# An attention and feed-forward layer on eight cores: the first weight product summed in another order, weight and x loads reordered, six w1 loads issued two steps later

## The reference, cut to what matters

```
x: (4, 4096, 1024) f32
h   = layernorm(x)
q,k,v = the three interleaved thirds of h @ W_qkv.T
attn  = softmax(q @ k.T / sqrt(1024));  out = (attn @ v) @ W_out.T
x   = x + layernorm(out)
f   = gelu(layernorm(x) @ w1 + b1) @ w2 + b2          # 1024 -> 4096 -> 1024
x   = x + layernorm(f * s)                           # s: renormalised top-2 router sum
```

## Time and profile before

| | |
|---|---|
| median of 3 runs | 1098.89 us |
| profiled execution | 1098.99 us, span of its slowest core (core 5) 1097.5 us |
| spans of the 8 cores | 1090.4 to 1097.5 us |
| TensorE busy | 1068.1 us (97%), 5192 matmuls |
| VectorE, ScalarE, GpSimd busy | 345.0, 316.7, 96.7 us |
| DMA | 110.03 MB, mean 100 GB/s |

### The profile page before, as it was taken

The page is one execution under the profiler, slowest core; times in us unless marked ns, Lnnn a source line. Parts: engine busy times, 40 slices in busy tenths (PEclk is TensorE's granted clock), DMA queues, the critical chain, the costliest instruction groups (busy, mean ns, idle before and its releaser), DMA issues.

```text
span 1097.5 us, 14077 instructions; the slowest of 8 cores (1090.4 to 1097.5 us)
## 1 busy us (share of the span) xinstructions
PE 1068.1 (97%) x5192; PEld 493.0 (45%) x5192; DVE 345.0 (31%) x713; ACT 316.7 (29%) x514; POOL 96.7 (9%) x171
## 2 busy tenths in 40 slices
PE   5999999999999999999999997999999999999996
PEld 2554444444444444444444443444444444444444
DVE  0563832333433333334433204023003300330033
ACT  0564432223332222223331222302430243014300
POOL 7220000000000000000000303010000000000000
PEclk9999999999999999999999998999999999999998
DMA  8999973443234445433349999974202220120012
GB/s 121 164 184 209 159 186 66 106 97 86 80 75 102 91 106 106 106 90 79 75 96 148 138 174 174 169 203 118 37 1 75 66 53 1 60 75 20 1 42 74
DMA packets 152867, 110.03 MB, mean 100 GB/s; under 512 B 117600, under 2 KB 128096, under 8 KB 152800
## 3 DMA queue, kind: packets, MB, share of 16 engines
q0 software_dynamic: 31120, 62.94, 29.3%
q1 hardware_dynamic: 121680, 46.20, 20.8%
HBM read 88.69 MB, written 25.17 MB: 104 GB/s over the span
## 4 chain that ended last, share of the span: by engine, by line
PE 89%; DMA 7%; POOL 2%; issue 1%; DVE 0%; SPq 0%; ACT 0%; POOLq 0%; DVEq 0%; ACTq 0%
PE pAll L116 88%; DMA x2s<-xf 4%; DMA wkb<-wk 2%; DMA pT<-pb 1%; PE pAll L120 1%; POOL wkb L110 1%; POOL wqb L110 0%; POOL w2b L110 0%; POOL w1b L110 0%; SPq L112 0%; DVE xf L649 0%; DVE yt L886 0%; ACT ub L588 0%; DVE xf L643 0%; POOLq L983 0%
## 5 line engine op out<-in xcount | busy, mean ns | idle before, releaser
L116 PE MATMUL pAll<-xnT,qt 128*128 128x512 bf16 x1024 | 225.3, 379 | 0.0
L116 PE MATMUL pAll<-xn,pT 128*128 128x512 bf16 x1024 | 223.6, 379 | 0.0
L116 PE MATMUL pAll<-x2T,w1b 128*128 128x512 bf16 x1024 | 222.6, 379 | 0.0
L116 PEld LDWEIGHTS pAll<-xn,pT 128*128 128x128 bf16 x1024 | 100.2, 98 | 120.8
L116 PEld LDWEIGHTS pAll<-xnT,qt 128*128 128x128 bf16 x1024 | 100.1, 98 | 120.9 <-issue 0.3
L116 PEld LDWEIGHTS pAll<-x2T,w1b 128*128 128x128 bf16 x1024 | 99.7, 98 | 120.1 <-issue 1.1
L528 DVE TENSOR_REDUCE nmx<-pAll 128x1 f32<-128x1024 f32 x64 | 78.1, 1222 | 180.0 <-PE pAll L116 180.0
L534 ACT ACTIVATE pb<-pAll,nmx 128x1024 bf16<-128x1024 f32 x64 | 71.3, 1114 | 168.8 <-DVE nmx L528 168.8
L116 PE MATMUL pAll<-w2b,h1b 128*128 128x512 bf16 (+1 forms) x528 | 113.3, 373 | 0.0
L116 PE MATMUL pAll<-w2b,h1a 128*128 128x512 bf16 (+1 forms) x528 | 113.3, 373 | 0.0
L116 PEld LDWEIGHTS pAll<-w2b,h1a 128*128 128x128 bf16 x528 | 51.7, 98 | 59.1
(11 more groups left out here) (86 smaller groups left out, 577.2 us busy)
## 6 DMA issues: line engine op xcount, KB each, us to landing
xf<-xo POOLq DMA_DIRECT2D x16, 512.0 KB, 4.5
x2s<-xf POOLq DMA_DIRECT2D x16, 512.0 KB, 2.9
w1b<-w POOLq DMA_DIRECT2D x8, 1024.0 KB, 23.3
w2b<-w POOLq DMA_DIRECT2D x8, 1024.0 KB, 32.9
x2r<-x2s POOLq DMA_DIRECT2D x16, 512.0 KB, 4.8
y<-yt SPq DMA_DIRECT2D x15, 512.0 KB, 2.7
xn<-xo POOLq DMA_DIRECT2D x16, 256.0 KB, 30.0
xn<-xr POOLq DMA_DIRECT2D x16, 256.0 KB, 56.2
```

The lines of the kernel that those rows point to most:

```text
L116: e.matmul(o, l, m, start=f, stop=s), after, sig)
```

## The change

Six things are edited.

1. Load order. Wq and Wk pieces come as q0 k0, q1 k1, q2 k2, q3 k3 (first column half of Wk), then second-half pieces 0 to 3, then q4 to q7 each with its second-half piece, then first-half pieces 4 to 7, with x tile 0 behind piece 4 and x tile 1 ahead of piece 7.
2. A's first column half is summed over c 0 to 3 in 8 banks and put aside, scaled, as f32 in `part` (in the place of x tiles 16 to 23). Then the whole second half is summed. Then c 4 to 7 of the first half, and the two parts are added: even blocks by one VectorE operation, odd ones by ScalarE into `rest` and an add on GpSimd. TensorE's transpose of tile 1 moves out of A.
3. `fetch_x(16)` waits for these eight results.
4. The first q' group goes tile by tile: 20 pieces of one tile (8 matmuls of 128 columns), four pieces of two tiles (256 columns) and one block of four.
5. `norm_next` calls take other places in the first group; `rot` starts elsewhere.
6. w1 loads 2 to 7 are issued behind `out_proj(12)`, `finish_a(12)` and `finish_b(12)`, not ahead of them.

```diff
--- before.py
+++ after.py
@@ -214,23 +214,33 @@
 
     t_q, t_k, t_x = [], [[], []], []
 
-    def fetch_x(t):
+    def fetch_x(t, after=()):
         src = xo if t < NQT else xr
         row = (t % NQT) * 128
-        t_x.append(DG(xn[:, t * H:(t + 1) * H], src[row:row + 128, :]))
+        t_x.append(DG(xn[:, t * H:(t + 1) * H], src[row:row + 128, :], after))
 
     t_id = DS(ident[:, :], idb[:, :])
     t_b1 = DS(b1f[:, :], b1r[:, :])
+    def fetch_k(c, half):
+        row = slice(c * 128, (c + 1) * 128)
+        k = slice(half * 512, (half + 1) * 512)
+        t_k[half].append(DG(wkb[:, c * H + half * 512:c * H + half * 512 + 512],
+                            wk[row, k]))
+
     for c in range(HC):
-        row = slice(c * 128, (c + 1) * 128)
-        t_q.append(DG(wqb[:, c * H:(c + 1) * H], wq[row, :]))
-        t_k[0].append(DG(wkb[:, c * H:c * H + 512], wk[row, 0:512]))
-    for c in range(HC):
-        row = slice(c * 128, (c + 1) * 128)
-        t_k[1].append(DG(wkb[:, c * H + 512:(c + 1) * H], wk[row, 512:H]))
+        t_q.append(DG(wqb[:, c * H:(c + 1) * H],
+                      wq[c * 128:(c + 1) * 128, :]))
+        fetch_k(c, c // 4)
         if c == 3:
+            for n in range(4):
+                fetch_k(n, 1)
+    for c in range(4, HC):
+        if c == 7:
+            fetch_x(1)
+        fetch_k(c, 0)
+        if c == 4:
             fetch_x(0)
-    for t in range(1, NQT):
+    for t in range(2, NQT):
         fetch_x(t)
 
     t_xT = [None] * NKT
@@ -317,56 +327,90 @@
         t_xT[t] = free[b] = A(lambda e: e.copy(dst, src), [tok])
 
 
+
+
     t_am = [[None] * HC, [None] * HC]
-
-    def am_part(i, half, c, b, aft):
+    part = [at(f"part{i}", 512, F32, R2 + 32 * KB + i * 2 * KB)
+            for i in range(HC)]
+    rest = [at(f"rest{i}", 512, F32, R2 + 48 * KB + i * 2 * KB)
+            for i in range(4)]
+    t_part = [None] * HC
+
+    def am_step(i, half, c, b, first, last, aft):
         return MM(bank[b], wqb[:, c * H + i * 128:c * H + (i + 1) * 128],
                   wkb[:, c * H + half * 512:c * H + (half + 1) * 512],
-                  c == 0, c == HC - 1, aft, c == HC - 1)
-
-    def am_out(i, half, b, done):
-        o = am[:, i * H + half * 512:i * H + (half + 1) * 512]
-        if half == 1 or i % 2 == 0:
-            t = A(lambda e: e.mul(o, bank[b], 0.03125), [done])
+                  first, last, aft, last)
+
+    def scaled(eng, o, b, tok):
+
+        if eng == "act":
+            return A(lambda e: e.mul(o, bank[b], 0.03125), [tok])
+        return V(lambda e: e.tensor_scalar(o, bank[b], 0.03125, None,
+                                           ALU.mult), [tok])
+
+    def am_cols(i, half):
+        return am[:, i * H + half * 512:i * H + (half + 1) * 512]
+
+    for c in range(4):
+        for i in range(HC):
+            tok = am_step(i, 0, c, i, c == 0, c == 3,
+                          [t_q[c], t_k[0][c]] if i == 0 else ())
+            if c == 3:
+                t_part[i] = free[i] = scaled("dve" if i % 2 else "act",
+                                             part[i][:, :], i, tok)
+    for rows in (range(4), range(4, HC)):
+        for c in range(4):
+            for i in rows:
+                aft = [t_k[1][c]] if i == 0 else []
+                if c == 0:
+                    aft.append(free[i])
+                am_step(i, 1, c, i, c == 0, False, aft)
+    for c in range(4, HC):
+        for i in range(HC):
+            tok = am_step(i, 1, c, i, False, c == HC - 1,
+                          [t_q[c], t_k[1][c]] if i == 0 else ())
+            if c == HC - 1:
+                t_am[1][i] = free[i] = scaled("dve" if i % 2 else "act",
+                                              am_cols(i, 1), i, tok)
+    norm_next()
+    last_bank = (0, 1, 2, 3, 4, 5, 7, 6)
+    t_last = [None] * HC
+
+    def last_step(i, c):
+        aft = [t_k[0][c]] if i == 0 else []
+        if c == 4:
+            aft.append(free[last_bank[i]])
+        t_last[i] = am_step(i, 0, c, last_bank[i], c == 4, c == HC - 1, aft)
+
+    def last_out(i):
+
+        b, o, p = last_bank[i], am_cols(i, 0), part[i][:, :]
+        if i % 2 == 0:
+            t_am[0][i] = free[b] = V(lambda e: e.scalar_tensor_tensor(
+                o, bank[b], 0.03125, p, ALU.mult, ALU.add),
+                [t_last[i], t_part[i]])
         else:
-            t = V(lambda e: e.tensor_scalar(o, bank[b], 0.03125, None,
-                                            ALU.mult), [done])
-        t_am[half][i] = free[b] = t
-
-    for c in range(HC):
-        for i in range(HC):
-            tok = am_part(i, 0, c, i, [t_q[c], t_k[0][c]] if i == 0 else ())
-            if c == HC - 1:
-                am_out(i, 0, i, tok)
+            r = rest[i // 2][:, :]
+            free[b] = scaled("act", r, b, t_last[i])
+            t_am[0][i] = G(lambda e: e.tensor_tensor(o, r, p, ALU.add),
+                           [free[b], t_part[i]])
+
+    for c in range(4, 7):
+        for i in range(7):
+            last_step(i, c)
+    norm_apply()
+    transpose_x(0)
     norm_next()
-    for c in range(HC):
-        for i in range(4):
-            aft = [t_k[1][c]] if i == 0 else []
-            if c == 0:
-                aft.append(free[i])
-            tok = am_part(i, 1, c, i, aft)
-            if c == HC - 1:
-                am_out(i, 1, i, tok)
-    norm_apply()
-    for i in range(4, HC):
-        b = i if i < 6 else i - 6
-        for c in range(HC):
-            tok = am_part(i, 1, c, b, [free[b]] if c == 0 else ())
-        if i == 4:
-            transpose_x(0)
-            norm_next()
-            am_out(i, 1, b, tok)
-        elif i == 5:
-            am_out(i, 1, b, tok)
-            norm_next()
-        elif i == 6:
-            am_out(i, 1, b, tok)
-            transpose_x(1)
-        else:
-            norm_next()
+    for i in range(7):
+        last_step(i, 7)
+        if i == 0:
+            last_out(0)
             norm_apply()
-            am_out(i, 1, b, tok)
-    t_amm = tok
+    for c in range(4, HC):
+        last_step(7, c)
+    t_amm = t_last[7]
+    for i in (1, 6, 3, 2, 5, 4, 7):
+        last_out(i)
 
 
     t_v, t_o = [], []
@@ -380,7 +424,7 @@
             wo[c * 128:(c + 2) * 128, :].rearrange("(c p) o -> p c o", p=128),
             [t_amm]))
     for t in range(NQT, NKT):
-        fetch_x(t)
+        fetch_x(t, t_am[0] if t == NQT else ())
     t_rw = DG(rwb[:, :], rwr[:, :])
 
     t_qt, t_s = {}, {}
@@ -391,7 +435,7 @@
 
 
     t_qs = [None] * NQT
-    rot = [2]
+    rot = [0]
 
     def next_free():
         b = rot[0] % 6
@@ -444,33 +488,55 @@
         free[b] = A(lambda e: e.copy(o, bank[b]), [tok, t_qs[4], t_qs[8]])
         t_bm.append(free[b])
 
-    norm_at = {0: (4, 5, 6), 1: (0, 3, 6), 3: (4, 7)}
+
+
+    norm_at = {1: (0, 3, 6), 3: (4, 7)}
     for g in range(NQG):
         toks = []
         if g == 0:
-            three = [next_free() for j in range(3)]
-            q_part(0, 0, three[0], 0, 2)
+            first = [(4, 0), (5, 1), (6, 3), (7, 2), (0, 4), (1, 5)]
+            for j, b in first[:3]:
+                q_part(0, j, b, 0, 1)
+            transpose_x(1)
+            q_part(0, 7, 2, 0, 1)
+            norm_next()
+            norm_next()
+            norm_apply()
+            for j, b in first[:4]:
+                q_part(0, j, b, 1, 1)
+            q_part(0, 0, 4, 0, 2)
             transpose_x(2)
-            transpose_x(3)
+            q_part(0, 1, 5, 0, 2)
+            for j, b in first:
+                q_part(0, j, b, 2, 1)
+                if j == 4:
+                    transpose_x(3)
             norm_next()
-            q_part(0, 1, three[1], 0, 2)
-            q_part(0, 2, three[2], 0, 2)
-            for j, b in enumerate(three):
-                q_out(0, j, b, q_part(0, j, b, 2, 2), toks)
-            transpose_after = (2, 4, 5, 6)
+            for n, (j, b) in enumerate(first):
+                q_out(0, j, b, q_part(0, j, b, 3, 1), toks)
+                if n in (1, 3):
+                    norm_next()
+                if n == 2:
+                    transpose_x(4)
+            transpose_x(5)
+            q_out(0, 2, 0, q_part(0, 2, 0, 0, 4), toks)
             norm_next()
-            transpose_x(4)
-        else:
-            transpose_after = (0, 2, 4, 6)
+            transpose_x(6)
+            norm_apply()
+            q_part(0, 3, 1, 0, 2)
+            transpose_x(7)
+            q_out(0, 3, 1, q_part(0, 3, 1, 2, 2), toks)
+            norm_next()
+            rot[0] = 3
         if g == 2:
             norm_apply()
-        for j in range(3 if g == 0 else 0, HC):
+        for j in range(HC if g else 0):
             if j in norm_at.get(g, ()):
                 norm_next()
             b = next_free()
             q_out(g, j, b, q_part(g, j, b, 0, 4), toks)
-            if g < 3 and j in transpose_after:
-                transpose_x(4 * (g + 1) + transpose_after.index(j))
+            if g < 3 and j in (0, 2, 4, 6):
+                transpose_x(4 * (g + 1) + j // 2)
```

(6 more changed lines are left out.)

## The result

The changed kernel takes **1103.18 us** (median of 9 runs, 1100.58 to 1109.56), the kernel before 1098.74 on the same chip (9 runs): a ratio of 1.0047, 95% interval 1.0028 to 1.0066. It is within 2%, as I had given it 0.96, but it is slower beyond that interval, and 6 us above the top of my range (1097.0). The profiled execution took 1103.18 us for a span of 1101.6 on its slowest core, which is core 5 again. So core 5 can be held against core 5: +4.1 us. It is no typical core, though: the other seven have spans of 1091.9 to 1099.4, and cores 1, 2 and 3 are 0.9 to 4.0 us faster than before.

What follows compares the result with a forecast made beforehand. TensorE was taken as the bound nearly everywhere, with the DMA engines busy through the first 145 us. Core 5: 1097.5 - 8.7 + 1.8 = 1090.6; another core perhaps slowest at 1091.0; forecast 1092.4 us, range 1089.2 to 1097.0.

Steps and rivals of the forecast that it cites:

- stall ahead of `out_proj(15)` and its clock: TensorE's 6.69 us wait before `out_proj(15)` and the lowered clock behind it go: -8.7 us on core 5.
- start of the first scores: TensorE loses its lead from A by tile 8's transpose and lags: +1.8 us on core 5.
- waits for w2 in the first ffn2: The last w2 piece still lands in time for ffn2: cost 0, up to 2 us for the range.
- the slack is between 0 and 2: a cost of 0: w2's 4.5 us of slack, with need 8.7 us earlier and the stream 4 to 6 us quicker.
- They start at 607.9 as before, or 1 to 3 us later.: w1 pieces 2 to 7 wait for `pT(15)`, which may be delayed 1 to 3 us by tile 12's two stores.
- I put that at 4 to 6 us: Gain of the w2 stream from losing the pause after 660.5 and tile 12's 0.75 MB: 4 to 6 us.
- ScalarE's burst: First q' group: six bank copies and more come in a lump, so VectorE idles some 2 us after tile 7's Ln.
- The last keys: Before chunk 3 of the first scores: a TensorE lead wins at most 1.0 us on core 5, 0 on core 2.
- The lowered clock: Rival: the wait at tile 8 lowers TensorE's clock, costing 2.0 to 2.25 us, total 1094.6; chance 0.23.
- Slower: Rival: `uT(15)`, queued against w1 and w2, lands late and `out_proj(15)` waits again, up to 1100.7; chance 0.04.
- Absorbed: Rival: VectorE keeps up, TensorE's lead of up to 1.4 us is lost at the last keys, 1090.7; chance 0.27.
- The sign that I had named: If `out_proj(15)` waits for a DMA, or ffn2 for w2, the account of the second place is wrong.

Runs made afterwards that it cites:

- start alone: The changed kernel with edit 6 undone, the w1 loads back in their old place: 1103.86 us, ratio 1.0051 to the kernel before.
- w1 alone: The kernel before with only edit 6, w1 loads 2 to 7 issued later: 1095.31 us, ratio 0.9973.
- Experiment 5: The kernel before with the last four of B's 16 blocks summing one of eight chunks (28 matmuls left out, B wrong there): 1097.79 us, ratio 0.9998.
- repaired start: Edits 1 to 5 with `rot` 4 in place of 3 and the statistics of tiles 8 and 9 ahead of tile 7's application: 1100.96 us, ratio 1.0018.

## Why the prediction was wrong

Core 5, the step as predicted and as the trace has it:

| step | predicted | measured |
|---|---|---|
| stall ahead of `out_proj(15)` and its clock | -8.7 | -8.9 |
| start of the first scores | +1.8 | +4.4 |
| waits for w2 in the first ffn2 | 0, up to 2 | +8.7 |
| span | -6.9 | +4.1 |

The measured -8.9 is the start of the first ffn2, 695.20 against 699.67, with the lag of 4.4 taken out. The +8.7 is how much longer the first ffn2 takes: the 8.0 of waits, and 0.16 us more at each of the four than the idle time says.

**The step that failed: "the slack is between 0 and 2: a cost of 0".** It failed in two places.
- "They start at 607.9 as before, or 1 to 3 us later." They started 9.85 us later. 4.71 of it is the lag: `pT(15)` is issued at 601.81 instead of 597.10. The other 5.1 is the transpose, landing after 15.3 us instead of 10.2. Its issue, and its landing after and before:
```profile
601.81 10.35 SPq L112 DMA_TRANSPOSE pT<-pb  x1
```
```profile
pT<-pb SPq DMA_TRANSPOSE x1, 15.3
```
```profile
pT<-pb SPq DMA_TRANSPOSE x1, 10.2
```
The stores at 607.32 and 611.32 now share the engines with it. The start alone has the same lag and no stores there, and its transposes take 10.7 to 12.0 us on the eight cores; with the stores it is 12.6 to 15.3 in the changed kernel and 11.3 to 17.9 with w1 alone. On the seven other cores the transpose takes 1.4 to 2.5 us longer than before, so my 1 to 3 us were right for them. The lag moves TensorE's need for w2 as well, so that it takes only 0.3 us of the slack. The transpose takes all of its 5.1, and I had left even my own 1 to 3 us out.
- "I put that at 4 to 6 us", for a w2 stream without the pause and the 0.75 MB. From the first of the six w1 pieces to the last w2 data were 111.5 us before (607.87 to 719.4), and are 110.3 now (617.72 to 728.02). The stream won 1.2 us. On the other cores it is between 0.8 us longer and 6.1 us shorter than before (2.7 shorter on average over the eight). The two stores of tile 12 had landed before it began (by 615.4 and 617.1), so it did carry less; why it is not shorter by 4 to 6 is not shown. On core 5 the six w1 pieces take 53.2 us to land, against 51.2 before, and the rest 57.0 against 60.1.

For core 5 the wait can be put together from these numbers. It is a sum of measured shifts, and does not explain the stream's length. ffn2 comes 8.9 us earlier, against the lag; w1 is 0.3 later beyond the lag and 5.1 by the transpose; the stream is 1.2 shorter; the slack was 4.5: 8.9 + 0.3 + 5.1 - 1.2 - 4.5 = 8.6, where 8.7 was measured. The experiments bear the cause out, a w1 that starts late: with the w1 edit alone the waits are there, and with w1 let go earlier they fall to 0 to 3.4, or 0 to 2.7 in the changed kernel.

**The start, +4.4 instead of +1.8.** The mechanism was right: A at 40.98 (42.4 predicted), VectorE behind ScalarE's burst with an idle of 1.96 ("some 2 us"), waits of 1.29 and 2.83 (1.5 and 3.5), tile 8 at 67.19 (67.5). That the last number came so close is in part luck: tile 1's statistics began at 37.89 and not at 39.1, and from there to tile 8 VectorE took 4.6 us more than the 24.7 of work that I had counted, where I had allowed 3.7. My own waits didn't add up either: from 61.0 to 67.5 are 6.5 us, and 1.5 and 3.5 make 5.0; small waits for ScalarE's tile copies, 1.6 in all, were not in them. Two terms were missing. The clock after the wait at tile 8 was my rival with 0.23: 1.7 us here, none on cores 1 and 3, 1.3 to 1.7 on the rest. And the bank: the 1.03 us stands in the code as `rot[0] = 3` and not in any row of before. I had followed each engine's work through group 0 and not the hand-over of banks behind it. The fast 128-column pieces held: 24 in 1.34 us, 56 ns each. The 81 ns that the Trainium skill ("TensorE: Matmul & The Clock Gate", Back-to-back issue gap) gives for them don't fit this trace. GpSimd's adds cost TensorE nothing, at 1.26 us each.

**The last keys.** I had given a lead of TensorE at most 1.0 us. Experiment 5 found 1.5 at the end for the mean core and next to nothing for the slowest, though keys can land 2 to 4 us earlier than I had said. That a lag is paid from there on held too: chunk 3 waited on no core of the changed kernel. What core 5 doesn't show is that the start costs other cores more. In the profiles of the start alone the first scores start 4.8 us later on average over the eight cores (3.6 on core 5) and the first ffn2 5.6 later; in those of the repaired start, 1.0 and 2.0 later. In between, waits for keys ahead of chunk 3 are gone, but `out_proj(15)` costs more: the wait there is 5.3 and 4.7 us on average, against 4.4 before, and every core works at a lowered clock behind it, where cores 4 and 6 of the kernel before did not (waits of 3.07 and 2.53). Why the wait grows isn't known. In the repaired start's profile it and its clock are 1.2 of the 2.0 us.

**The rivals.** None was it. The lowered clock came, as one term of three. "Slower" put the wait at `uT(15)`, which held nothing up; the wait came one consumer later, at w2. "Absorbed" fell with VectorE, which did not keep up, and would have needed w2 on time as well. The sign that I had named, ffn2 waiting for w2, is the one that showed.

## What to carry to other kernels

When a stall goes, work out when the next load of the same queue is needed and when it lands, from the first byte of the stream: its start, its length and the slack must each have a number, and a shift once conceded must be carried to the end of the sum. An order that sends one transfer earlier lets it share the engines with whatever ran there before; ask whether that one gates the stream. Read every core before you explain the slowest: here the spans change by -4.0 to +4.1 us from core to core, and the slowest is the one that had the longest waits. And where a change redistributes PSUM banks, check the bank of the last block of one stage against the first of the next.

## What the runs showed of the hardware

- A DMA transpose of 1 MB, taking 10.2 to 12.4 us in the kernel before, with two 1 MB weight loads issued some 15 us ahead of it, takes 21.9 to 24.0 when a third one is in flight as it is issued (and two stores beside it; these alone make it 11.3 to 17.9), and 40.5 to 45.0 when five more are queued as well before its issue has ended. It isn't known whether the queue or the engines do this; a run with another queue for w1 wasn't made.
- Waits of the same length left TensorE's clock alone or lowered it: at tile 8, 2.83 us cost nothing or 1.3 to 1.7 us; at tile 7, 2.2 us cost nothing or 1.0 to 1.4; while 3.07 before `out_proj(15)` and 3.22 before chunk 3 (experiment 5, core 5) cost nothing. The length of one wait doesn't decide it. What does is open.
